# Shifted-window attention on one core: both low halves of the probabilities go to GpSimd, and the stack DMA is issued before a reload

## The reference

```python
x = x + _L0_conv_ref(_gn(x), w_qkv, pos_emb, w_out, b_out)
# in _L0_conv_ref: x is rolled by (-3, -3), cut into windows of N = 49 tokens, 64 windows an image
dots = jnp.einsum('bhwid,bhwjd->bhwij', q, k) * scale
dots = dots + pos_emb[rel[:, :, 0], rel[:, :, 1]]     # and the masks of the shifted edges
attn = jax.nn.softmax(dots, axis=-1)
out = jnp.einsum('bhwij,bhwjd->bhwid', attn, v)
# then out @ w_out.T + b_out, rolled back by (3, 3)
```

## Time and profile before

| what | us |
|---|---|
| median of 3 runs | 4303.33 (4303.29 to 4307.44) |
| the profiled execution | 4301.36 |
| its span, first to last instruction | 4299.6 |
| PE busy | 4151.4 (97%) |
| DVE busy | 3717.4 (86%) |
| ACT busy | 2271.7 (53%) |
| POOL busy | 2223.2 (52%) |

### The profile page before, as it was taken

One profiled execution on the slowest core, in us unless ns is written; L12 is line 12 of the kernel. 1 busy time (PEld: TensorE's weight loads), 2 busy tenths in 40 slices (PEclk: granted clock), 3 DMA queues, 4 the chain that ended last, 5 costly groups with the idle time before them and its releaser, 6 DMA issues.

```text
span 4299.6 us, 166334 instructions
## 1 busy us (share of the span) xinstructions
PE 4151.4 (97%) x65384; PEld 2982.5 (69%) x65384; DVE 3717.4 (86%) x9283; ACT 2271.7 (53%) x4225; POOL 2223.2 (52%) x1933
## 2 busy tenths in 40 slices
PE   3999999999999999999999999999999999999998
PEld 1677767777777767777677677777777777776776
DVE  5888888888888888888888888888888888888887
ACT  0555555555555555555555555555555555555554
POOL 1555555555555555555455555555555555555554
PEclk9999999999999999999999999999999999999999
DMA  4445444444444444444444444444534444444442
GB/s 125 102 111 126 106 112 117 110 114 112 113 118 106 115 120 103 113 125 106 112 116 112 113 113 111 120 110 108 123 101 113 125 105 112 117 111 113 102 105 62
DMA packets 231108, 479.07 MB, mean 111 GB/s; under 512 B 39009, under 2 KB 140898, under 8 KB 222818
## 3 DMA queue, kind: packets, MB, share of 16 engines
q1 hardware_dynamic: 230338, 468.43, 43.1%
HBM read 159.99 MB, written 77.07 MB: 55 GB/s over the span
## 4 chain that ended last, share of the span: by engine, by line
PE 65%; SPq 12%; DVE 10%; DMA 6%; ACT 4%; issue 4%; POOL 0%; DVEq 0%; ACTq 0%; POOLq 0%
PE ps_pj L1102 22%; PE ps_post L1198 12%; PE ps_pj L1098 9%; SPq L466 8%; DMA stack<-qk 6%; PE ps_post L1189 4%; PE ps_sa L1136 3%; PE ps_st L1166 3%; PE ps_pv L1182 3%; PE ps_pv L1181 2%; PE ps_pv L1180 2%; PE ps_st L1136 2%; ACT ph L681 2%; PE ps_pj L1086 2%; SPq L401 2%
## 5 line engine op out<-in xcount | busy, mean ns | idle before, releaser
L575 POOL TENSOR_TENSOR rb<-tq,cst 128x588 bf16<-128x588 bf16 x512 | 606.4, 1184 | 1698.7 <-ACT tq L668 1698.7
L607 ACT ACTIVATE qk<-ps_pj 128x392 f16<-128x392 f32 x768 | 381.9, 497 | 953.9 <-PE ps_pj L1102 947.8
L681 ACT ACTIVATE ph<-ps_st,sc 64x588 f16<-64x588 f32 x1024 | 772.2, 754 | 6.5
L1102 PE MATMUL ps_pj<-xh,wh 128*128 128x392 f16 x2304 | 765.9, 332 | 6.9 <-POOL xl L539 4.1
L1102 PE MATMUL ps_pj<-xh,wl 128*128 128x392 f16 x2304 | 765.0, 332 | 0.0
L1102 PE MATMUL ps_pj<-xl,wh 128*128 128x392 f16 x2304 | 764.8, 332 | 0.0
L878 DVE TENSOR_TENSOR qk<-ps_pj,qk 128x392 f16<-128x392 f32 x768 | 433.1, 564 | 383.7 <-ACT qk L607 377.6
L561 POOL TENSOR_TENSOR pl<-pf,ph 64x588 f16<-64x588 f32 x512 | 650.3, 1270 | 149.6 <-POOL rb L575 133.7
L547 POOL TENSOR_TENSOR xb<-xs,bout 98x384 f32<-98x384 f32 x512 | 513.8, 1004 | 107.9 <-DMA out<-xb 85.6
L966 DVE TENSOR_TENSOR pl<-pf,ph 64x588 f16<-64x588 f32 x512 | 529.0, 1033 | 0.1
L1180 PE MATMUL ps_pv<-vh,ph 128*128 128x33 f16 x6144 | 516.3, 177 | 1.6 <-DVE pl L966 1.6
(11 more groups left out here) (107 smaller groups left out, 8887.3 us busy)
## 6 DMA issues: line engine op xcount, KB each, us to landing
stack<-qk SPq DMA_DIRECT2D x1536, 147.0 KB
sx<-in_x SPq DMA_DIRECT2D x66, 1176.0 KB
xs<-in_x SPq DMA_DIRECT2D x384, 84.0 KB
out<-xb SPq DMA_DIRECT2D x384, 84.0 KB
xs<-in_x SPq DMA_DIRECT2D x384, 63.0 KB
out<-xb SPq DMA_DIRECT2D x384, 63.0 KB
xs<-in_x SPq DMA_DIRECT2D x128, 66.0 KB
out<-xb SPq DMA_DIRECT2D x128, 66.0 KB
```

The source lines that it names most:

```text
L575: nc.gpsimd.tensor_tensor(rb[:, :, :, :], tq[:, :, :].unsqueeze(2).broadcast_to([128, 2, HH, N]), const_of("own_head").unsqueeze(1).unsque ...
L681: e = nc.scalar.activation(ph[rows, :, w * PAD:w * PAD + N].rearrange("p (a h) n -> p a h n", a=2), ps_st[rows, :, 0:HH * N].rearrange("p ...
L1102: m = mm(ps_pj[bank][:, 0:RT].rearrange("p (w n) -> p w n", w=NW), wa[:, c, o:o + 128], xa[:, b, c, :, 0:N], **on)
```

## The change

The low half that VectorE made is now made by GpSimd, which makes both, one after the other, first partitions 0 to 63. GpSimd waits for each to be done before it goes on (it waited for its one half before too). The first condition of the two, `s_rb`, `s_ph` and `s_pv`, is as it was. VectorE's instruction and its waits are gone. On SP, the stack's wait and its 12 DMAs stood at the start of ticks 2 and 6; now they stand in ticks 1 and 5, after the store and before the reload of that tick. What they wait for is the same.

```diff
@@ SP, step(tk), for k in range(8)
-                    if p == 2 and not (tk.last and odd):
-                        stack_row(1 - odd, unit_count(tk, 4 * odd + 1, "k", 2), 8 * n + 4 * odd)
...
                     if not (tk.first and k < 3):
                         store(t - 3, tk, k - 3)
+                    if p == 1 and not (tk.last and odd):
+                        stack_row(1 - odd, unit_count(tk, 4 * odd + 1, "k", 2), 8 * n + 4 * odd)
                     if not (tk.last and k + LEAD >= 8):
                         reload(tk if k + LEAD < 8 else ahead(tk), (k + LEAD) % 8)
@@ GpSimd, split_probabilities(t, spread)
                 need(pool, s_pv, t)
-                nc.gpsimd.tensor_tensor(pl[PAD:, :, PAD:PAD + N], pf[PAD:, :, :], ph[PAD:, :, PAD:PAD + N],
-                                        ALU.subtract).then_inc(s_pl[1], 1)
+                for w in range(2):
+                    rows, cols = slice(w * PAD, (w + 1) * PAD), slice(w * PAD, w * PAD + N)
+                    nc.gpsimd.tensor_tensor(pl[rows, :, cols], pf[rows, :, :], ph[rows, :, cols],
+                                            ALU.subtract).then_inc(s_pl[w], 1)
+                    pool.wait_ge(s_pl[w], t + 1)
@@ GpSimd, step
                         split_probabilities(t - 1, t + 1)
-                        pool.wait_ge(s_pl[1], t)
@@ VectorE: split_probabilities and its two calls
-            def split_probabilities(t):
-                dve.wait_ge(s_ph, t + 1)
-                need(dve, s_pv, t)
-                nc.vector.tensor_tensor(pl[0:PAD, :, 0:N], pf[0:PAD, :, :], ph[0:PAD, :, 0:N],
-                                        ALU.subtract).then_inc(s_pl[0], 1)
```

More of the change, by code:

```diff
@@ L1015, in step @@
                     between(5)
-                    if not (tk.first and k < 1):
-                        split_probabilities(t - 1)
                     if not (tk.last and k >= 4):
@@ L1033, in _ @@
             output(end - 3, 5)
-            split_probabilities(end - 1)
             attended_low(end - 2)
```

## The result

The changed kernel takes 4455.7 us (median of 4 runs, 4455.2 to 4458.05) against 4303.4 us before: 1.0353 times as long, 95% interval 1.0335 to 1.0371. The loss is 152.3 us. The profiled execution spans 4453.7 us, 154.1 us more than before.

What follows compares the result with a forecast made beforehand. PE sets the pace, so only its few waits count. From 4301.4 us: + 162.5 (126 junctions of 1.29) - 22.5 (VectorE) - 23 (stack) + 1.3 (last tick) = 4419.7, as median 4421 us; range over the cases 4370 to 4478.

Steps and rivals of the forecast that it cites:

- the forecast's own case: The main case: 4421 us, own range 4395 to 4450, chance 0.55.
- The chain behind `rb`: GpSimd from `rb` to q0's weight load: two `pl` before `xl` make 5.18 us of 4.24, 0.94 us lost per row.
- The wait in front of `mt`: VectorE in ticks 3 and 7: L945 waits for GpSimd's `residual` on the port, delaying `shift_rows` 0.35 us per row.
- my upper value: If the cast before L945 also waits for `residual`: 0.55 us per row, the sum some 25 us higher.
- my second rival: GpSimd's chain longer: cast blocked (0.55) and self-wait 0.29 (0.21 more), or `xl` stays 1.31; 4473 us, chance 0.20.
- What DVE gains: In the 15 finishing steps, two `pl` of 0.75 us leave VectorE's queue: 22.5 us gained, possibly 0 to 49.5.
- The stack: Stack DMAs start 1.6 us sooner, so nearly all PE waits for them go: 23 us gained, or nothing if hidden under `xl`.
- What `pf` waits for: ScalarE's `pf` waits for both halves, some 0.4 us later in ticks 3 and 4; nothing follows for PE.
- GpSimd as a bound: GpSimd is not the bound: 1.35 us more per tick goes into a third of idle time; only its latency counts.
- No port wait: Rival: L945 does not wait for `residual`, so a row costs 0.94 us, 118.8 us in all; 4378 us, chance 0.18.
- off PE's path: Rival, faster: the halves do not delay PE at q0 in ticks 0 and 4, only gains remain; 4258 us, chance 0.03.
- PE's clock: Rival: new gaps step PE's clock down; 1.2 GHz for a tenth of the time adds 430 us, chance 0.01.

Runs made afterwards that it cites:

- low part of x first: Changed kernel, but in ticks 3 and 7 GpSimd makes the low part of x ahead of both halves of `pl`: 4374.5 us, ratio 1.0169.
- the stack alone: Kernel before with only the stack's DMAs moved, between store and reload of ticks 1 and 5: 4283.4 us, ratio 0.9956.
- Divided by ticks: Changed kernel, but GpSimd makes both halves only in ticks 0, 1, 4 and 5; VectorE keeps its half in the others: 4276.2 us, 0.9934.
- one half left out: Kernel before with VectorE's half of the low probabilities not made and nobody waiting for it; stack not moved: 4283.6 us, 0.9958.
- later sums: Changed kernel, but `residual` of ticks 2 and 6 is made in ticks 3 and 7, behind `xl`: 4392.0 us, 1.0202.
- The best version: Changed kernel, VectorE keeping its half in ticks 2, 3, 6, 7; there `xl` before `pl` in 3, 7; `residual` of 2, 3, 6, 7 one tick later: 4250.2 us.

## Why the prediction was right

The sign and the place held, and so did the size in the main: 4421 us forecast, 4456 measured, within 4370 to 4478, though 6 us above the range of the forecast's own case (4395 to 4450). The forecast loss, 118 us, is 34 us under the measured one. By its steps:

- *The chain behind `rb`*, 5.18 us instead of 4.24: measured 5.18 in the junction shown. The halves at 1.27, the gap at 0.08 and `xl` at 0.9 were each right. The steps give 0.91 us a junction for the 0.94 of the sum, and the run with the low part of x first shows that this order is the cause.
- *The wait in front of `mt`*, 0.35 us a row: this is the term that was mis-sized. I let L945 wait for `residual` and not the cast. It is the cast that waits (0.92 us), and L947 follows at once, one instruction later: from `mw` to the end of `mt` it is 1.53 us instead of 0.83. PE had some 0.15 us of slack there, and about 0.55 remain, my upper value; the steps give 0.61. That is half of my second rival ("cast blocked"); its other half, a self-wait of 0.29 us between the halves, did not come. The Trainium skill's rule ("SBUF — State Buffer", Who interferes with whom) that a cast in a 2-port mode shares the lock decided right here, and the trace now agrees with it (0.92 us for a cast of 0.18). The text said that no row shows a cast that met POOL. Among the rows listed that is so, but the trace of the kernel before has one, of its 512, in the first step's tick 3 (timelines of DVE and POOL, kernel before):

```profile
134.87 0.91 DVE L941 CAST mt<-mw 128x24 bf16<-128x24 f32 x1
134.74 1.00 POOL L547 TENSOR_TENSOR xb<-xs,bout 98x384 f32<-98x384 f32 x1
```

The longest of the 512 would have settled the term at 0.55. With 0.55 the sum would have been 126 x 0.20 = 25 us higher, 4446 us.
- *What DVE gains*, 22.5 us: from the stack alone to the changed kernel a finishing step grew by 1.46 us, 1.58 less than an ordinary one, 24 us over 15. The size is right, the mechanism only in part, and that is luck. Divided by ticks, where no junction loses anything, the finishing steps won 0.75 us each, 11 us and not 22.5. Another part is a loss that they were spared: in their ticks 7 the cast doesn't meet `residual`, about 9 us at 0.61 each. And the run with one half left out won nothing in them.
- *The stack*, 23 us: 17.4 us in the kernel before; in the changed one the two versions differ by 0.3 us, the wrong way, which is nothing. The text had this too ("nothing if those waits now end inside the new wait for `xl`"). As a term it was still consistent, because the junction was priced against one without a stack wait: it is a part of the loss given back, not a gain of this edit.
- *What `pf` waits for.* ScalarE's `pf` now waits for `pl` 202.8 us in 257 waits, against 22.3 in 27 for VectorE's half before. PE's waits at `attend` only went from 1.6 to 3.5 us. The text had it so: nothing follows.
- *The rivals.* GpSimd as a bound was not needed: it is 62% busy. "No port wait" is refuted by the cast and by the 64 us that the later sums gave back, "off PE's path" by the waits for `xl`. The sum of "no port wait" has a slip: 126 x 0.94 is 118.4 and not 118.8. PE's clock stayed at 1.00 in all the stretches shown.

With the measured terms the sum is 126 x 1.52 - 17.4 - 24 + 1.3 = 151.4 us, against 152.3 measured. The terms of the steps come from the same trace, so this shows that nothing large lies outside the junctions and the finishing steps; it is no second proof of their causes.

## What to carry to other kernels

When work moves to an engine with idle time, don't add up its busy share. Look at what stands behind the new instruction in its queue, and who needs that first: here a low part of x that was ready 0.11 us before the weight load that needed it turned 1.35 us of extra work on an engine that was half idle into a wait at nearly every one of 126 junctions. Then look at who shares a port with it: small VectorE instructions on the path to PE grew fivefold under GpSimd's long ones. Order alone, with all of the work left on GpSimd, gave back 81 us of the 152 at `xl` or 64 at the sums; the two together were not run, so how far order alone goes is open. The best version, 53 us faster than the kernel before, has the stack's move and a division of the work too: it makes three quarters of the changed kernel's GpSimd `pl` instructions and puts the sums, which nobody needs soon, where neither `xl` nor `mt` is near. And before a term is set by a typical row, look at the longest one of its group: one cast in 512 told the price.

## What the runs showed of the hardware

- A cast of 128 x 24 elements from fp32 to bf16, both in SBUF, took 0.18 us alone and 0.92 us when it came just behind the start of a GpSimd sum of 98 x 384 elements, and ended 0.03 us after GpSimd's instruction. `mw`, with two SBUF inputs, did likewise (0.18 to 0.89 us).
- It goes the other way as well: GpSimd's `xl` takes 0.9 us alone and 1.31 to 1.44 us when VectorE's `pl`, with two SBUF inputs, waits ahead of it. Once VectorE's half was gone, the mean of all `xl` was 908 ns.
- A waiting VectorE instruction got in between two GpSimd ones that followed each other: in the changed kernel `mw` and the cast each waited for one (0.37 and 0.92 us). None waited for two: of the 512 each, the longest `mw` took 0.907 us and the longest cast 0.925.
